# Graph layer behind a layer norm: the mean's subtraction and the clipping done by GpSimd, with a third input buffer

## The chip, the core and the metric

One core of a Trainium2 chip runs the whole program. The metric is the device time of one execution in microseconds (us), the median over several runs. Engines are named as in the profile's rows: PE is TensorE, DVE VectorE, ACT ScalarE, POOL GpSimd, SP SyncE.

## The reference

`x` has 128 matrices of 120 x 1024, `adj` is a symmetric 120 x 120 matrix. Cut to what matters:

```python
h = jnp.maximum(_layernorm(x, axis=-1), 0.0)
Ln = dinv[:, None] * Lap * dinv[None, :]          # from adj
_, U = jnp.linalg.eigh(Ln)
agg = jnp.einsum('vn,bvd->bnd', U, h)
out = relu(agg @ W1 + b1) @ W2 + b2
# non-local block: th, ph, g projections, max pooling by 2,
# softmax(theta phi) g, projection wo, batch norm, residual -> z
return x + einsum('nv,bvd->bnd', U, z) + z
```

`_layernorm` divides by the root of the variance, which is positive, so clipping can come ahead of the division. The kernel works with `max(x - mean, 0)`, multiplies it by `W1`, and applies the factor `rstd` to the product later.

## The kernel before, in words

There are two parts. The first, the setup, holds two pieces of work that run at the same time. The second is a loop over the 128 matrices with the attention, paced by TensorE; it starts when the setup is done and is not touched by the change.

**The eigenvectors.** A 120 x 120 matrix is brought to tridiagonal form by 118 reflections (`reflect` on VectorE, L983, and on TensorE, L694). Of each, GpSimd does five operations on single numbers in `shift` (L429: a sign, a root by a power, a product, a gate). They wait for the vector `u` that VectorE writes in L1015 of the reflection before (`u_ready`) and for its norm (`s2_ready`). The product of L436 (`du_ready`) lets VectorE go on at L990. Then VectorE alone computes eigenvalues and eigenvectors (`minors` and `count`, L1066 to L1110, three times, and a recurrence at L1157 to L1168). Once, at L1122, it waits for a small product of TensorE (L760, `grid_count`). VectorE's last instruction of the setup is L1274 (`setup_done`), which waits for all of `P1` too. Meanwhile the reflections are put together to a matrix in 19 pieces (`factor` on ScalarE, L555, and TensorE, L719; `masked` on GpSimd, L443).

**The normalised matrices.** For each of the 128 matrices: SP loads it into one of two buffers `xin` (`load`, L325); ScalarE sums it with the factor -1/D (`b_sum`, L509), clips `x - mean` at zero into `frelu` (`b_relu`, L514), and squares and sums for the variance (`b_sq`, L519). TensorE transposes `frelu` in eight pieces (`transposes`, L663), ScalarE copies them out of PSUM (`b_ft`, L524), TensorE multiplies by `W1` (`product`, L674), ScalarE keeps the product in `P1` (`b_p1`, L531). On GpSimd, `rstds` (L459) turns the sums of squares into `rstd`, in two halves of 64 matrices.

**The order.** Each engine has one queue, written out by hand. TensorE's part of a matrix is cut into six pieces (`norm_piece`, L685): two of transposes, four of the product of the matrix two before. Reflection `k` is followed by pieces up to number `(k - 2) * 39 // 10`, so that 448 are done with the last reflection; the rest, up to 780, follow without reflections between them. The small product of L760 stands ahead of piece 546 (`GRID_AT * 6`), and `factor` begins at matrix 93. ScalarE goes in slots (`slot`, L535): clear and square matrix `k`, copy the transposes of `k - 2`, sum `k + 1`, keep the product of `k - 4`. At the end GpSimd sets the first row of `xt` to zero (L475, `xt_free`); SP waits for that before its four small loads (L338, L339), and TensorE waits for these ahead of the loop (L898). The root of the sum of squares of the eigenvectors is taken by GpSimd in L469.

Of the kernel before, what the change touches and what calls it, by code (L numbers as in the profile page):

```python
# [46 lines left out]
def build(nc, x, adj, W1, b1, W2, b2, g_w, g_b, th_w, th_b, ph_w, ph_b, wo_w, wo_b,  # L47
          bn_gamma, bn_beta, bn_mean, bn_var, out):
    ctx = ExitStack()
    with ctx:  # L50
# [6 lines left out]
        def sem(name):  # L57
            return ctx.enter_context(nc.semaphore(name))
# [21 lines left out]
        rstd = sb("rstd", [128, B])  # L80
# [4 lines left out]
        with early:  # L85
            def eb(name, shape, dt=F32):
                return sb(name, shape, dt, early)
            xin = eb("xin", [N, 2, D])
            frelu = eb("frelu", [N, 2, D])
            junkx = eb("junkx", [N, D], BF16)  # L90
            fT = eb("fT", [128, 2, KC * N])
            W1s = eb("W1s", [128, KC, H])
            lns = eb("lns", [N, 2, 1])
            QA = eb("QA", [N, 2 * N])
            strict = eb("strict", [N, N])
            sub = eb("sub", [N, N])
# [67 lines left out]
            wyA, wyB = xt[:, 0, :], xt[:, 1, :]  # L164
            part = lambda t, i: t[:, i * 128:(i + 1) * 128]
            wyC, wyCT, wyG, wyL, wyX, wyY, wyP, wyM = [part(wyA, i) for i in range(8)]
            wyS = part(wyB, 0)


        pst = sb("pst", [128, 2, H])  # L170
# [46 lines left out]
        grid_below = sem("grid_below")  # L217
        grid_count = sem("grid_count")
        xcol_ready = sem("xcol_ready")
        x_in = [sem(f"x_in{i}") for i in range(2)]  # L220
        mean_done = sem("mean_done")
        relu_done = sem("relu_done")
        sq_done = sem("sq_done")
# [37 lines left out]
        def late(eng, s, count):  # L261

            if not isinstance(count, int) or count > 0:
                eng.wait_ge(s, count)

        def rounds(eng, lo, hi, body):

            assert (hi - lo) % 2 == 0
            with eng.Fori(lo // 2, hi // 2) as i:
                body(i * 2, 0)  # L270
                body(i * 2 + 1, 1)
# [29 lines left out]
        def _(sp):  # L301
            sp.dma_start(LA[:, 0:N], adj).then_inc(adj_in, 16)
            n = 0
# [18 lines left out]
            sp.dma_start(P1[N:N + 1, :].rearrange("a (b j) -> a b j", j=H),  # L322
                         b1.rearrange("(a c j) -> a c j", a=1, c=1).to_broadcast([1, B + 1, H])).then_inc(b1_in, 16)

            def load(k, par):  # L325

                late(sp, sq_done, k - 1)
                sp.dma_start(xin[:, par, :], x[bass.ds(k, 1), :, :].rearrange("a n d -> n (a d)")).then_inc(x_in[par], 16)
            load(0, 0)
            load(1, 1)  # L330
            rounds(sp, 2, B, load)


            sp.wait_ge(consts, 1)
# [46 lines left out]
        def _(pool):  # L381
# [44 lines left out]
            pool.wait_ge(dve_out, 1)  # L426
            pool.tensor_tensor(colA[:, 6:7], colA[:, 5:6], colA[:, 10:11], ALU.pow).then_inc(pool_out, 1)

            def shift(k):  # L429

                pool.wait_ge(u_ready, k + 1)
                chain(pool.tensor_scalar(sc[:, SGN:SGN + 1], u[:, 1:2], 0.0, 2.0, ALU.is_ge, ALU.mult))
                chain(pool.tensor_scalar(sc[:, SGN:SGN + 1], sc[:, SGN:SGN + 1], -1.0, None, ALU.add))
                pool.wait_ge(s2_ready, k + 1)
                chain(pool.tensor_tensor(sc[:, ROOT:ROOT + 1], sc[:, S2:S2 + 1], sc[:, 11:12], ALU.pow))  # L435
                pool.tensor_tensor(sc[:, DU:DU + 1], sc[:, SGN:SGN + 1], sc[:, ROOT:ROOT + 1], ALU.mult).then_inc(du_ready, 1)  # L436
                pool.tensor_scalar(sc[:, GATE:GATE + 1], sc[:, XN:XN + 1], TINY, -1.0, ALU.is_gt, ALU.mult).then_inc(gate_ready, 1)

            for k in range(STEPS):
                shift(k)  # L440


            def masked(level):  # L443
# [9 lines left out]
                pool.affine_select(out=view(wyL), in_=view(wyL), compare_op=ALU.is_ge, fill=0.0, base=size - 1,  # L453
                                   pattern=[[2 * size, blocks], [0, size]], channel_multiplier=-1).then_inc(wy_mask, 1)

            for level in range(7):
                masked(level)

            def rstds(a, z):  # L459

                pool.wait_ge(sq_done, z)
                chain(pool.tensor_scalar(rstd[0:N, a:z], rstd[0:N, a:z], 1.0 / D, LN_EPS, ALU.mult, ALU.add))
                pool.tensor_tensor(rstd[0:N, a:z], rstd[0:N, a:z], colA[:, 10:11].to_broadcast([N, z - a]),
                                   ALU.pow).then_inc(rstd_done, 1)
            rstds(0, B // 2)


# [3 lines left out]
            pool.tensor_tensor(colA[:, 8:9], colA[:, 7:8], colA[:, 10:11], ALU.pow).then_inc(pool_out, 1)  # L471


            pool.wait_ge(wy_ps, WY_P(7) + 1)
            pool.memset(xt[0:1, :, :], 0.0).then_inc(xt_free, 1)  # L475
            rstds(B // 2, B)
            pool.wait_ge(rstd_done, 2)
            pool.wait_ge(setup_done, 1)

# [26 lines left out]

        @block.scalar
        def _(act):
            def b_sum(s, par):  # L509
                act.wait_ge(x_in[par], s * 8 + 16 - 8 * par)  # L510
                act.activation(junkx[:, :], xin[:, par, :], ACT.Copy, scale=-1.0 / D,
                               accum_out=lns[:, par, 0:1]).then_inc(mean_done, 1)

            def b_relu(s, par):  # L514
                act.wait_ge(mean_done, s + 1)
                late(act, tr_done, s - 1)
                act.activation(frelu[:, par, :], xin[:, par, :], ACT.Relu, bias=lns[:, par, 0:1]).then_inc(relu_done, 1)

            def b_sq(s, par):  # L519
                act.wait_ge(mean_done, s + 1)  # L520
                act.activation(junkx[:, :], xin[:, par, :], ACT.Square, bias=lns[:, par, 0:1],
                               accum_out=rstd[0:N, bass.ds(s, 1)]).then_inc(sq_done, 1)

            def b_ft(s, par):  # L524
                act.wait_ge(tr_done, s + 1)
                late(act, w1_done, s - 1)
                for j in range(2):
                    last = act.activation(fT[:, par, j * 4 * N:(j + 1) * 4 * N], ps_T[par][:, j, 0:4 * N], ACT.Copy)
                last.then_inc(ft_done, 1)

            def b_p1(s, par):  # L531
                act.wait_ge(w1_done, s + 1)
                act.activation(P1[0:N, bass.ds(s * H, H)], ps_m[par][0:N, 0:H], ACT.Copy).then_inc(p1_done, 1)  # L533

            def slot(k, par):  # L535
                fixed = isinstance(k, int)
                if not fixed or k < B:
                    b_relu(k, par)
                    b_sq(k, par)
                if not fixed or 0 <= k - 2 < B:  # L540
                    b_ft(k - 2, par)
                if not fixed or k + 1 < B:
                    act.wait_ge(sq_done, k + 1)
                    b_sum(k + 1, 1 - par)
                if not fixed or 0 <= k - 4 < B:
                    b_p1(k - 4, par)

            act.wait_ge(consts, 1)
            b_sum(0, 0)
            def keep(*copies):  # L550

                for out, in_, scale in copies:
# [27 lines left out]
                    act.wait_ge(wy_ps, WY_P(7) + 1)  # L580
                    keep((QA[:, N:2 * N], ps_V[0:N, 128:128 + N], 1.0))

            for k in range(4):
                slot(k, k % 2)
            rounds(act, 4, WY_SLOT, slot)
            for k in range(WY_SLOT, B + 4):
                slot(k, k % 2)
                if k < WY_SLOT + WY_STEPS:
                    factor(k - WY_SLOT)


# [59 lines left out]
        def _(pe):  # L651
# [60 lines left out]
            pe.wait_ge(params, 16 * PARAMS)  # L712
            done = 0
            for k in range(STEPS):
                wanted = max(0, (k - LN_LEAD) * LN_RATE[0] // LN_RATE[1])
                reflect(k, done, wanted)
                done = wanted

# [621 lines left out]
PARAMS = 15  # L1340
XN, S2, ROOT, GATE, SGN, REC, DU, RG, AC = range(9)
LN_RATE, LN_LEAD, LN_BEHIND = (39, 10), 2, 1
GRID_AT = 91
WY_SLOT, WY_STEPS = 92, 19
WY_T, WY_G = 1, 4
# [38 lines left out]
```

## Time and profile before

| | |
|---|---|
| median of 3 runs | 3405.35 us (3404.03 to 3417.64) |
| profiled execution | 3414.81 us |
| its span in the profile | 3412.6 us |
| PE busy | 3235.3 us (95%) |
| DVE busy | 2318.8 us (68%) |
| ACT busy | 2411.8 us (71%) |
| POOL busy | 1942.8 us (57%) |

The profile is of one execution. Durations in it are to be held against its own 3414.81 us. A group of instructions is shown with its line, engine, operation, the tiles it writes and reads, the shapes, the count, then busy time and the mean of one, and the idle time of the engine just before them with what ended it. In a timeline each row has start and length in us; in brackets is how long the engine had been idle, and who released it.

### The profile page before, as it was taken

How to read it: one execution, taken by the hardware profiler on the slowest of the kernel's cores; microseconds unless marked ns; L12 is line 12 of the kernel's file. 1: busy time of each engine (PE TensorE's matmuls, PEld its weight loads, DVE VectorE, ACT ScalarE, POOL GpSimd, SP SyncE). 2: the span in 40 equal slices, each digit the busy share in tenths (PEclk: the TensorE clock that was granted, in tenths of full speed). 3: DMA queues.
4: the chain of work that ended last, by engine and by line, in shares of the span. 5: the costliest groups of instructions: out<-in, count | busy, mean ns of one | idle time of the engine just before them, and what ended most of it. 6: DMA issues, size and time to landing. Idle time of an engine off the chain costs nothing.

```text
span 3412.6 us, 66625 instructions
## 1 busy us (share of the span) xinstructions
PE 3235.3 (95%) x16512; PEld 2604.2 (76%) x16512; DVE 2318.8 (68%) x6125; ACT 2411.8 (71%) x4381; POOL 1942.8 (57%) x2069
## 2 busy tenths in 40 slices
PE   6888887779999999999999999999999999999997
PEld 4777776657777777777777777777777777777775
DVE  5777778976666666666666666666666666666664
ACT  4777889957666666667666666676666666667665
POOL 4333320126666666666666666666666666666665
PEclk9998999989999999999999999999999999999998
DMA  2233334412222222222222222222222222222222
GB/s 79 79 82 82 93 95 114 112 41 65 70 74 77 70 70 76 70 70 70 76 75 70 70 76 70 70 70 76 75 70 70 75 70 70 70 77 74 70 71 69
DMA packets 111579, 256.28 MB, mean 75 GB/s; under 512 B 47500, under 2 KB 49797, under 8 KB 111493
## 3 DMA queue, kind: packets, MB, share of 16 engines
q1 hardware_dynamic: 111493, 255.25, 27.2%
q8 instruction: 40, 0.66, 0.1%
q14 instruction: 46, 0.38, 0.0%
HBM read 190.69 MB, written 63.44 MB: 74 GB/s over the span
## 4 chain that ended last, share of the span: by engine, by line
PE 81%; DVE 11%; POOL 3%; issue 3%; ACT 1%; DVEq 0%; ACTq 0%; POOLq 0%
PE ps_M L781 8%; PE ps_M L782 8%; PE ps_M L783 8%; PE ps_S L858 7%; PE ps_E L781 7%; PE ps_O L781 7%; PE ps_O L783 7%; PE ps_E L782 7%; PE ps_E L783 7%; PE ps_O L782 7%; PE ps_M L842 3%; PE ps_m L680 1%; POOL sc L435 1%; PE ps_S L863 1%; PE ps_M L797 1%
## 5 line engine op out<-in xcount | busy, mean ns | idle before, releaser
L487 POOL TENSOR_TENSOR p_lo<-p,p_hi 128x512 fp32r<-128x512 f32 x1024 | 1374.3, 1342 | 936.0 <-ACT p_hi L639 931.8
L634 ACT ACTIVATE p<-ps_E 128x512 f32<-128x512 f32 x1024 | 613.5, 599 | 333.0 <-PE ps_E L783 307.6
L1324 DVE TENSOR_REDUCE nmx<-ps_S 128x1 f32<-128x512 f32 x1024 | 658.3, 684 | 130.2 <-PE ps_S L858 127.3
L639 ACT ACTIVATE p_hi<-p 128x512 fp32r<-128x512 f32 x1024 | 647.0, 632 | 32.7
L781 PE MATMUL ps_E<-o_hi,Q_hi 123*128 123x512 f32 x1024 | 426.9, 417 | 0.0
L781 PE MATMUL ps_O<-p_hi,v_hi 128*121 128x512 f32 x1024 | 406.9, 397 | 4.6 <-POOL p_lo L487 4.6
L783 PE MATMUL ps_O<-p_lo,v_hi 128*121 128x512 f32 x1024 | 406.3, 397 | 0.0
L782 PE MATMUL ps_E<-o_hi,Q_lo 123*128 123x512 f32 x1024 | 404.2, 395 | 0.0
L783 PE MATMUL ps_E<-o_lo,Q_hi 123*128 123x512 f32 x1024 | 404.0, 394 | 0.0
L782 PE MATMUL ps_O<-p_hi,v_lo 128*121 128x512 f32 x1024 | 403.8, 394 | 0.0
L1304 DVE TENSOR_REDUCE gf<-ps_M 128x256 f32<-128x512 f32 x256 | 177.0, 691 | 261.9 <-PE ps_M L783 261.9
L858 PE MATMUL ps_S<-Q_hi,o_hi 122*128 122x512 f32 x1024 | 347.3, 399 | 2.7 <-DVE nmx L1324 1.5
L494 POOL TENSOR_TENSOR y<-y,acc 121x512 f32<-121x512 f32 x256 | 329.3, 1286 | 13.5 <-DVE y L1332 13.5
L781 PE MATMUL ps_M<-o_hi,Chi 122*128 122x512 f32 (+1 forms) x768 | 313.0, 408 | 2.5 <-DVE o_lo L1289 1.5
L680 PE MATMUL ps_m<-W1s,fT 128*120 128x128 f32 x2048 | 296.9, 292 | 9.6 <-ACT P L533 9.6
L783 PE MATMUL ps_M<-o_lo,Chi 122*128 122x512 f32 (+1 forms) x768 | 302.4, 394 | 0.0
L782 PE MATMUL ps_M<-o_hi,Clo 122*128 122x512 f32 (+1 forms) x768 | 302.1, 393 | 0.0
L680 PEld LDWEIGHTS ps_m<-W1s,fT 128*120 128x120 f32 x2048 | 254.4, 192 | 29.2 <-issue 23.9
L1295 DVE TENSOR_REDUCE phf<-ps_M 128x256 f32<-128x512 f32 x256 | 175.6, 686 | 128.9 <-PE ps_M L783 128.9
L858 PEld LDWEIGHTS ps_S<-Q_hi,o_hi 122*128 122x128 f32 x1024 | 193.2, 189 | 77.7 <-ACT mrow L624 27.0
L606 ACT ACTIVATE o_hi<-ps_M 120x512 fp32r<-120x512 f32 x256 | 153.2, 598 | 138.7 <-PE ps_M L783 138.7
L781 PEld LDWEIGHTS ps_E<-o_hi,Q_hi 123*128 123x128 f32 x1024 | 193.7, 189 | 49.6 <-issue 6.7
(355 smaller groups left out, 6101.3 us busy)
## 6 DMA issues: line engine op xcount, KB each, us to landing
rbc<-r_dram SPq DMA_DIRECT2D x128, 484.0 KB
xin<-in_x_dram SPq DMA_DIRECT2D x128, 480.0 KB, 4.2
xt<-in_x_dram SPq DMA_DIRECT2D x128, 480.0 KB, 5.0
out_dram<-y SPq DMA_DIRECT2D x128, 480.0 KB, 3.8
o_hi<-mrow SPq DMA_DIRECT2D x256, 2.0 KB
dcol<-y SPq DMA_DIRECT2D x128, 4.0 KB, 2.0
r_dram<-rcol SPq DMA_DIRECT2D x128, 4.0 KB, 1.4
W1s<-in_L_gnn_W_dram SPq DMA_DIRECT2D x1, 512.0 KB, 4.1
```

What stands on the lines that cost most here:

```text
L487: pool.tensor_tensor(p_lo[:, c % 4, :], p[:, c % 4, :], p_hi[:, c % 4, :].bitcast(F32), ALU.subtract).then_inc(plo_sb, 1)
L494: pool.tensor_tensor(y[:, par, f], y[:, par, f], acc[:, par, f], ALU.add).then_inc(y_sb, 1)
L634: act.activation(p[:, c % 4, :], ps_E[c % 2][:, :], ACT.Exp).then_inc(p_sb, 1)
L639: act.activation(p_hi[:, c % 4, :], p[:, c % 4, :], ACT.Copy).then_inc(phi_sb, 1)
L680: last = mm(ps_m[par][0:N, 0:H], fT[:, par, c * N:(c + 1) * N], W1s[:, c, :], start=(c == 0), stop=(c == KC - 1))
L781: mm(dst, whi, mhi, start=start, stop=False)
L782: mm(dst, wlo, mhi, start=False, stop=False)
L783: return mm(dst, whi, mlo, start=False, stop=stop)
L858: mm(ps_S[SBANK[c]][:, :], o_hi[0:NA, par, c * 128:(c + 1) * 128], Q_hi[0:NA, par, :], start=True, stop=True).then_inc(S_ps, 1)
L1295: dve.tensor_reduce(phf[:, j * 256:(j + 1) * 256], ps_M[BANK["ph" + piece[2]]][:, :].rearrange("p (m t) -> p m t", t=2), AX.X, ALU.max).th ...
L1304: dve.tensor_reduce(gf[:, j * 256:(j + 1) * 256], ps_M[BANK["g" + piece[2]]][:, :].rearrange("p (m t) -> p m t", t=2), AX.X, ALU.max).then ...
L1324: dve.tensor_reduce(nmx[:, c:c + 1], ps_S[SBANK[c]][:, :], AX.X, ALU.max, negate=True).then_inc(max_sb, 1)
```

## The change

GpSimd computes `max(x + lns, 0)` with one TENSOR_SCALAR (`relu`), where `lns` holds the negative mean. ScalarE's `b_relu` is gone. On GpSimd the operations stand behind `shift(k)` while there are reflections, placed by the count of TensorE's pieces (76 of them), and the 52 others follow, with `masked` between them. `xin` has three buffers, `lns` four columns. A load waits for the square and the clearing of the matrix three before. ScalarE's sum of the next matrix stands ahead of the copies. The loops of SP and ScalarE over matrices are written out. `junkx`, the unused output of the sums, lies in `xt`. The first `rstds` follows the last `relu`, the second stands ahead of the fill of `xt`.

```diff
-            xin = eb("xin", [N, 2, D])
+            xin = eb("xin", [N, 3, D])
-            junkx = eb("junkx", [N, D], BF16)
-            lns = eb("lns", [N, 2, 1])
+            lns = eb("lns", [N, 4])
+            junkx = wyB[0:N, D // 2:D].bitcast(BF16)
...
-            def load(k, par):
-
-                late(sp, sq_done, k - 1)
-                sp.dma_start(xin[:, par, :], x[bass.ds(k, 1), :, :].rearrange("a n d -> n (a d)")).then_inc(x_in[par], 16)
-            load(0, 0)
-            load(1, 1)
-            rounds(sp, 2, B, load)
+            def load(k):
+
+                late(sp, sq_done, k - 2)
+                late(sp, relu_done, k - 2)
+                sp.dma_start(xin[:, k % 3, :], x[k:k + 1, :, :].rearrange("a n d -> n (a d)")).then_inc(x_in[k % 3], 16)
+            for k in range(B):
+                load(k)
...
+            def relu(s):
+
+                pool.wait_ge(mean_done, s + 1)
+                late(pool, tr_done, s - 1)
+                pool.tensor_scalar(frelu[:, s % 2, :], xin[:, s % 3, :], lns[:, s % 4:s % 4 + 1], 0.0, ALU.add,
+                                   ALU.max).then_inc(relu_done, 1)
...
+            cleared = 0
             for k in range(STEPS):
                 shift(k)
+                while cleared < (placed(k) - 4) // 6 + 2:
+                    relu(cleared)
+                    cleared += 1
...
-            for level in range(7):
-                masked(level)
...
+            for s in range(cleared, B):
+                relu(s)
+                if s >= WY_SLOT + 3 and (s - WY_SLOT - 3) % 2 == 0 and (s - WY_SLOT - 3) // 2 < 7:
+                    masked((s - WY_SLOT - 3) // 2)
             rstds(0, B // 2)
...
+            rstds(B // 2, B)
             pool.wait_ge(wy_ps, WY_P(7) + 1)
             pool.memset(xt[0:1, :, :], 0.0).then_inc(xt_free, 1)
-            rstds(B // 2, B)
...
-            def b_relu(s, par):
-                act.wait_ge(mean_done, s + 1)
-                late(act, tr_done, s - 1)
-                act.activation(frelu[:, par, :], xin[:, par, :], ACT.Relu, bias=lns[:, par, 0:1]).then_inc(relu_done, 1)
...
+            def slot(k):
+                if k < B:
+                    b_sq(k)
+                if k + 1 < B:
+                    b_sum(k + 1)
+                if 0 <= k - 2 < B:
+                    b_ft(k - 2, k % 2)
+                if 0 <= k - 4 < B:
+                    b_p1(k - 4, k % 2)
...
+def placed(k):
+
+    return max(0, (k - LN_LEAD) * LN_RATE[0] // LN_RATE[1])
```

## Rows read from the trace of the kernel before

**Rows 1.** Busy time of each engine in stretches, granted TensorE clock, DMA share, GB/s

```profile
20.00:482.00 462.00, 401.69 (x2936) 335.44 (x2935) 339.17 (x2121) 334.73 (x601) 167.89 (x590) 0.94 0.31 82
482.00:549.00 67.00, 49.22 (x402) 43.98 (x401) 53.33 (x238) 66.61 (x124) 0.00 (x0) 1.00 0.43 111
```

**Rows 2.** Timeline, one reflection: start us, us, engine, line, operation [idle before <-releaser]

```profile
256.99 0.24 POOL L432 TENSOR_SCALAR sc<-u 1x1 f32<-1x1 f32 x1 [2.67 <-DVE u L1015]
...
258.47 0.15 DVE L990 TENSOR_TENSOR u<-sc,u 1x1 f32<-1x1 f32 x1
258.52 0.22 POOL L437 TENSOR_SCALAR sc<-sc 1x1 f32<-1x1 f32 x1
...
258.87 0.20 DVE L997 SCALAR_TENSOR_TENSOR sqj<-u,zw 1x63 f32<-1x63 f32 x1
...
260.71 0.24 POOL L432 TENSOR_SCALAR sc<-u 1x1 f32<-1x1 f32 x1 [1.98 <-DVE u L1015]
```

**Rows 3.** GpSimd's L432: its group (busy, mean ns | idle before), its last start

```profile
L432 POOL TENSOR_SCALAR sc<-u 1x1 f32<-1x1 f32 x118 | 29.2, 247 | 256.3 <-DVE u L1015 253.5 <-DVE u L979 2.8
...
478.61 0.21 POOL L432 TENSOR_SCALAR sc<-u 1x1 f32<-1x1 f32 x1 [1.67 <-DVE u L1015]
```

**Rows 4.** Timeline of ScalarE, one slot after the reflections

```profile
700.92 1.07 ACT L511 ACTIVATE junkx<-xin 120x1024 bf16<-120x1024 f32 x1
...
702.12 1.17 ACT L517 ACTIVATE frelu<-xin,lns 120x1024 f32<-120x1024 f32 x1
...
703.18 1.15 ACT L521 ACTIVATE junkx<-xin,lns 120x1024 bf16<-120x1024 f32 x1
...
705.21 1.07 ACT L511 ACTIVATE junkx<-xin 120x1024 bf16<-120x1024 f32 x1
```

**Rows 5.** Timeline of VectorE at L1122

```profile
549.21 0.22 DVE L1122 SCALAR_TENSOR_TENSOR pv<-ps_up,pv 120x1 f32<-120x1 f32 x1 [9.27 <-PE ps_up L760]
```

**Rows 6.** GpSimd's groups: fills, one-input and two-input operations

```profile
L494 POOL TENSOR_TENSOR y<-y,acc 121x512 f32<-121x512 f32 x256 | 329.3, 1286 | 13.5 <-DVE y L1332 13.5
...
L397 POOL MEMSET o_hi<- 32x2048 f32 x1 | 1.8, 1799 | 0.1
...
L397 POOL MEMSET Q_hi<- 32x1024 f32 x1 | 0.9, 946 | 0.1
...
L462 POOL TENSOR_SCALAR rstd<-rstd 120x64 f32<-120x64 f32 x2 | 0.5, 252 | 0.2
```

**Rows 7.** VectorE late beside GpSimd, first and last of eight; L1076: ns min/median/max

```profile
565.81 0.25 DVE L1082 TENSOR_TENSOR SP<-ST,SM 120x48 f32<-120x48 f32 x1
565.70 0.70 POOL L453 TENSOR_SCALAR_AFFINE_SELECT xt<-xt 128x64 f32<-128x64 f32 x1
...
613.71 0.24 POOL L462 TENSOR_SCALAR rstd<-rstd 120x64 f32<-120x64 f32 x1
613.72 0.29 DVE L1076 TENSOR_TENSOR ST<-SA,SP 120x48 f32<-120x48 f32 x1
...
L1076 DVE TENSOR_TENSOR ST<-SA,SP x177: 200/208/288, 491.1 to 635.1; 120x48 f32<-120x48 f32 x177
```

**Rows 8.** GpSimd begun behind VectorE, in the attention loop

```profile
1014.74 1.23 DVE L1332 TENSOR_TENSOR y<-y,rbc 121x1024 f32<-121x1024 f32 x1 [0.24 <-DMA rbc<-r_dram]
1015.51 1.60 POOL L487 TENSOR_TENSOR p_lo<-p,p_hi 128x512 fp32r<-128x512 f32 x1 [0.80 <-ACT p_hi L639]
```

**Rows 9.** GpSimd's power operation and a two-input operation of VectorE inside it

```profile
716.07 10.54 POOL L463 TENSOR_TENSOR rstd<-rstd,colA 120x64 f32<-120x64 f32 x1
...
724.73 1.22 DVE L1262 TENSOR_TENSOR W2lo<-W2f,W2hi 128x1024 fp32r<-128x1024 f32 x1
```

**Rows 10.** End of the setup: SP's last small load, its landing, the first matmul

```profile
717.61 0.60 SPq L339 DMA_DIRECT2D o_lo<-b2lo  x1
...
728.83 0.75 PE L797 MATMUL ps_M<-Uaug,pst 121*128 121x120 f32 x2 [3.50 <-POOL pst L482]
...
DMA to landing us min/median/max: 2.0/2.0/2.0
```

More of the change, by code:

```diff
@@ L219, in build @@
         xcol_ready = sem("xcol_ready")
-        x_in = [sem(f"x_in{i}") for i in range(2)]
+        x_in = [sem(f"x_in{i}") for i in range(3)]
         mean_done = sem("mean_done")
@@ L508, in _, with b_sum, b_sq @@
         def _(act):
[L509 to L512, printed above, removed]
-            def b_relu(s, par):
-                act.wait_ge(mean_done, s + 1)
-                late(act, tr_done, s - 1)
-                act.activation(frelu[:, par, :], xin[:, par, :], ACT.Relu, bias=lns[:, par, 0:1]).then_inc(relu_done, 1)
-            def b_sq(s, par):
-                act.wait_ge(mean_done, s + 1)
-                act.activation(junkx[:, :], xin[:, par, :], ACT.Square, bias=lns[:, par, 0:1],
-                               accum_out=rstd[0:N, bass.ds(s, 1)]).then_inc(sq_done, 1)
+            def b_sum(s):
+                act.wait_ge(x_in[s % 3], (s // 3 + 1) * 16)
+                late(act, sq_done, s)
+                late(act, relu_done, s - 3)
+                act.activation(junkx, xin[:, s % 3, :], ACT.Copy, scale=-1.0 / D,
+                               accum_out=lns[:, s % 4:s % 4 + 1]).then_inc(mean_done, 1)
+            def b_sq(s):
+                act.wait_ge(mean_done, s + 1)
+                act.activation(junkx, xin[:, s % 3, :], ACT.Square, bias=lns[:, s % 4:s % 4 + 1],
+                               accum_out=rstd[0:N, s:s + 1]).then_inc(sq_done, 1)
             def b_ft(s, par):
@@ L533, in b_p1 @@
                 act.activation(P1[0:N, bass.ds(s * H, H)], ps_m[par][0:N, 0:H], ACT.Copy).then_inc(p1_done, 1)
[L535 to L546, printed above, removed]
+            def slot(k):
[7 more added lines that the diff above has]
+                    b_p1(k - 4, k % 2)
             act.wait_ge(consts, 1)
-            b_sum(0, 0)
+            b_sum(0)
             def keep(*copies):
@@ L581, in factor @@
                     keep((QA[:, N:2 * N], ps_V[0:N, 128:128 + N], 1.0))
[L583 to L588, printed above, removed]
+            for k in range(B + 4):
+                slot(k)
+                if WY_SLOT <= k < WY_SLOT + WY_STEPS:
                     factor(k - WY_SLOT)
@@ L714, in _ @@
             for k in range(STEPS):
-                wanted = max(0, (k - LN_LEAD) * LN_RATE[0] // LN_RATE[1])
+                wanted = placed(k)
                 reflect(k, done, wanted)
```

## The prediction

> **What bounds the kernel now.** I read the stretches first. Between 20 and 482 us the 118 reflections run, TensorE taking 3.9 sixths of a normalised matrix beside each; from 482 us VectorE goes on alone with the eigenvalues while ScalarE and TensorE finish the other matrices, ScalarE busy 66.6 of 67 us [rows 1]. Behind 728 us lies the attention loop, untouched by the change. ScalarE's share invites the change, so the next question is whether anything waits for ScalarE.
>
> In the reflections nothing does. The timeline of one step shows a loop through VectorE and GpSimd alone: the four small operations of `shift` on GpSimd, then L990 to L1015 on VectorE, whose end releases L432 again, at 260.71 us after 256.99 us a step earlier [rows 2]. GpSimd rests between two shifts: 256.3 us over 118 steps, so 2.17 us each, 1.67 us in the last step [rows 3]. ScalarE is beside this loop.
>
> After 482 us ScalarE sets the pace of the matrices, one per 4.29 us (L511 at 700.92 and at 705.21), yet VectorE's own chain ends the setup. It waited for the matrices at one place, L1122: TensorE reached the small product of L760 only when 91 matrices were through, and VectorE stood for 9.27 us [rows 4, 5]. That is all of ScalarE's lateness that the end feels.
>
> **Part by part.** *ScalarE loses the clearing.* From L517's start to L521's is 1.06 us, so its slot falls from 4.29 to 3.23 us [rows 4]. After the last reflection 448 of 546 sixths before L760 are placed, so 16.3 matrices are left; at 3.3 us each they take 54 us and end at 536 us, before the 539.9 us at which VectorE began to wait (549.21 less 9.27) [rows 5]. Gain 9.3 us; the rest of the 52 x 1.06 us = 55 us is hidden by VectorE's chain, which is the next thing late. Were only half the speed-up realised, 3.8 us per matrix would end at 544 us and still save 5 us.
>
> *GpSimd gets 128 clearings*, 76 within the reflections (one in two steps of three, behind the shift, ahead of the next) and 52 after them. No row has this operation. GpSimd's fill of 1024 elements takes 0.946 us, of 2048 1.80 us, so 0.83 ns an element; a TENSOR_SCALAR of 64 takes 0.252 us; together 0.252 + 960 x 0.00083 = 1.05 us. The other end is the two-input form, 1.286 us per 512, so 2.57 us [rows 6]. I take 1.05 us, as it has one input like L462. That fits into GpSimd's rest even in the last step (1.67 us) [rows 3]: as occupation it costs nothing. Its waits (the mean, the transposes of two matrices earlier) were met four steps before by the placement, and it is wanted by TensorE over half a step later; the shift queued behind it, and through it VectorE's L990, is who would pay if not.
>
> *What it does to VectorE* is the large unknown. Between 488 and 645 us I compared the distance between successive starts in VectorE's repeated operations with its median. Eight of them on two SBUF tensors came 0.04 to 0.09 us late, 0.45 us in all, and each lay at the start of a small GpSimd operation that reads SBUF (first 565.81 us beside L453, last 613.72 us beside L462; the usual length is 0.208 us) [rows 7]. There are 16 such GpSimd operations of about 64 elements, as much reading together as one clearing. So a clearing costs VectorE 0.45 us if the misses count, and 0.45 x 16 / 8 = 0.90 us if it always finds VectorE reading two tensors; the whole 1.05 us is the upper end. In the other direction, GpSimd's L487, begun 0.77 us after VectorE's L1332, took 1.60 us, where the like-shaped L494 takes 1.286 [rows 6, 8]: the two do not pass each other freely. The lower end is nothing at all: during GpSimd's power operation of 10.54 us VectorE's two-input L1262 ran its 1.22 us undisturbed [rows 9]. That operation reads 64 elements in ten microseconds, the clearing 1024 in one, so it is nearer to [rows 7]. I take 0.85 us, since a long read always meets a VectorE that is in its chain.
>
> The sum of that: in the reflections the clearing begins behind L437, at 258.8 us in the step shown, and L997 at 258.87 us would be held [rows 2]; 76 x 0.85 = 64.6 us. TensorE's mean granted clock is 0.94 there over 402 us of work, so up to 0.06 x 402 = 24 us of it is work at the lower level [rows 1]; part shows as longer steps, and a longer VectorE chain hides it. I take a third, 8 us off (ends 0 and 24): 56.6. Afterwards 52 clearings, four of them beside reductions and thus free: 48 x 0.85 = 40.8 us.
>
> By the Trainium skill (SBUF — State Buffer, "Who interferes with whom") a VectorE instruction with two SBUF inputs and a GpSimd instruction that reads SBUF exclude each other for a whole instruction; the trace agrees in kind in [rows 7, 8] and not in [rows 9], and by that rule the sum would take 1.05 us per clearing.
>
> *Order at the end.* The second `rstds` now stands ahead of the fill that frees `xt`: L462 and L463 are 0.3 + 10.54 us. The last of SP's four small loads, issued at 717.61 us, lands 2.0 us later, at 719.6; 10.9 us later that is 730.5, against the first matmul's 728.83 [rows 9, 10]. TensorE waits for them: 1.7 us lost. The third buffer, the unrolled loops and `junkx` within `xt` cost nothing: the loads stay beside 4 steps of slack.
>
> Sum: 56.6 + 40.8 - 9.3 + 1.7 = +89.8 us on the profiled execution's 3414.8 us, 3504.6 us. That execution lay 9.5 us above the median of 3405.35 us, so I forecast **3495 us**.
>
> **Rivals.** *(a) The clearing hardly touches VectorE* (up to 0.15 us each), as [rows 9] suggest. Then -9.3 + 1.7 = -7.6 us: 3398 us, up to 3417 at 0.15 us. This is the one that ends not slower. It decides below about 0.2 us per clearing: 128 x 0.2 = 26 us, less 7.6. Chance 0.26.
>
> *(b) VectorE is held for all of each clearing*: 76 x 1.05 + 52 x 1.05 = 134 us, nothing absorbed, -7.6: 3532 us; absorbed as above, some 3515. For it: L487's delay [rows 8]. Against it: [rows 9]. Chance 0.16. It is the rule that the Trainium skill states on the page and in the section named above.
>
> *(c) Partial sharing*, 0.2 to 0.45 us each: 128 x 0.33 - 7.6 = +35, 3440 us. It is [rows 7] with the misses counted. Chance 0.14.
>
> *(d) The clearing is longer than GpSimd's rest.* At 2.57 us it overruns the mean rest of 2.17 us by 0.4 and the 0.1 us of dispatch: 76 x 0.5 = 38 us, less 7.6: 3436 us. Against: one input. Chance 0.05.
>
> *(e) ScalarE's relief matters within the reflections too*, by way of TensorE's queue: up to the 24 us above, so 3374 us. Nothing waits for ScalarE there. Chance 0.03. That the change does not do what it says I give nothing beyond this: the operation is in the diff with its semaphores.
>
> **Numbers.** The forecast has 0.36. A difference of 0.5%, 17 us, is about what a measurement of this kernel can tell. Faster by more: 0.03. Within: (a), 0.27. Slower: the rest, 0.70. The forecast's own range is 3450 to 3515; as (a) must be within, the range is 3396 to 3530 us.
>
> **What would show it.** Right: the last L432 starts some 57 us later than 478.61 us [rows 3]; steps with a clearing about 0.85 us longer than those without, the gap inside VectorE's L995 to L1015; L1122 without a wait; ScalarE idle from about 482 + 56 x 3.3 = 667 us, plus what the reflections grow; the first matmul waiting for the small loads. Wrong: steps of equal length with and without a clearing (then rival a), or L432 waiting for the clearing's end (rival d), or a stretch from the first matmul of the loop to the end of other length than now, 3412.6 - 728.8 = 2683.8 us [rows 10].

## The result, and the profile after

The changed kernel took a median of 3575.17 us (3574.13 to 3576.54, 4 runs), the kernel before in the same session 3411.49 us (3404.03 to 3420.24, 4 runs): a ratio of 1.048, interval 1.045 to 1.051. The forecast was 3495 us, the range ended at 3530 us: right in its sign, short by 80 us. The profiled execution took 3574.13 us, with a span of 3572.3 us, 159.7 us more than the 3412.6 of before.

The page of after, first its busy times, then two of its groups and the chain that ended last:

```profile
PE 3328.0 (93%) x16512; PEld 2692.3 (75%) x16512; DVE 2407.9 (67%) x6125; ACT 2292.2 (64%) x4253; POOL 2437.8 (68%) x2197
...
PEclk9777767996999999999999999999999999999998
...
PE 77%; POOL 11%; DVE 10%; issue 2%; DMA 0%; ACT 0%; POOLq 0%; SPq 0%; DVEq 0%; ACTq 0%
...
L433 POOL TENSOR_SCALAR frelu<-xin,lns 120x1024 f32<-120x1024 f32 x128 | 485.6, 3801 | 13.6 <-PE ps_T L673 6.4
```

Look at the last line first. One clearing takes 3.8 us on GpSimd in the mean (3.72 in the median), where I had taken 1.05 and bounded it at 2.57. GpSimd's busy time rises by 2437.8 - 1942.8 = 495 us, ScalarE's falls by 120. GpSimd now has 11% of the chain.

The stretches, cut at the last reflection and at the end of the setup, as in [rows 1]:

```profile
20.00:598.00 578.00, 494.37 (x2911) 418.87 (x2910) 382.53 (x2110) 260.55 (x523) 444.78 (x663) 0.74 0.24 64
598.00:886.00 288.00, 174.44 (x1438) 163.37 (x1438) 261.72 (x1187) 184.36 (x401) 239.64 (x86) 0.87 0.33 88
```

The reflections end near 598 us instead of 482, with GpSimd busy for 445 of 578 us and TensorE's granted clock at 0.74, where [rows 1] had 0.94 (the mean of the stretch; 1 is the level of 2.4 GHz, 0.5 that of 1.2 GHz). A step with a clearing, GpSimd's timeline, and then VectorE's in the same step:

```profile
260.43 0.22 POOL L439 TENSOR_SCALAR sc<-u 1x1 f32<-1x1 f32 x1
...
261.93 0.23 POOL L444 TENSOR_SCALAR sc<-sc 1x1 f32<-1x1 f32 x1
262.25 3.72 POOL L433 TENSOR_SCALAR frelu<-xin,lns 120x1024 f32<-120x1024 f32 x1
265.95 0.22 POOL L439 TENSOR_SCALAR sc<-u 1x1 f32<-1x1 f32 x1
```

```profile
262.26 0.28 DVE L997 SCALAR_TENSOR_TENSOR zw<-row,sc,ps_up 1x72 f32<-1x72 f32 x1
262.46 0.91 DVE L999 SCALAR_TENSOR_TENSOR srow<-u,sc 1x1 f32<-1x1 f32 x1
263.30 0.21 DVE L1001 SCALAR_TENSOR_TENSOR sqj<-u,zw 1x72 f32<-1x72 f32 x1
...
264.82 0.28 DVE L1019 SCALAR_TENSOR_TENSOR u<-cs,zw,rown 1x70 f32<-1x70 f32 x1
```

The next shift (L439, the old L432) starts in the instant in which the clearing ends, with no idle time before it, though VectorE had `u` ready at 265.10. The step is 265.95 - 260.43 = 5.52 us: 3.72 of clearing and 1.80 of shift, both on GpSimd's queue. VectorE is held as well, which means that its operation lasts longer beside one of GpSimd's (L999 takes 0.91 us, 0.20 in steps without a clearing), but it has the time: it is done 0.85 us before GpSimd is. So in this step the holding costs nothing, and the queue all.

L439's group and its last start, as in [rows 3]:

```profile
L439 POOL TENSOR_SCALAR sc<-u 1x1 f32<-1x1 f32 x118 | 27.7, 234 | 89.8 <-DVE u L1019 87.0 <-DVE u L983 2.8
...
596.88 0.22 POOL L439 TENSOR_SCALAR sc<-u 1x1 f32<-1x1 f32 x1
```

The waits between 20 and 598 us (who waited for whom: us in total, times, longest):

```profile
POOL sc L439 <- DVE u L1019: 87.0, 44, 2.9
DVE u L994 <- POOL sc L443: 40.2, 54, 1.8
```

GpSimd waited for `u` 44 times instead of 117. The last reflection began at 596.9 us, 118.3 us later than before's 478.6. Of the 76 clearings 75 lie between the first start at 20.2 and the last. The 75 steps with one took 5.51 to 5.78 us, 5.56 in the mean, and the other 42 took 3.81 in the mean, near the mean of all before, (478.6 - 20.2) / 117 = 3.92. So 75 x (5.56 - 3.92) = 123 us is the loss, less 42 x 0.11 = 5 us that the others gained.

The profiled execution of before was not one of its quickest. The six kernels of the experiments below that have no clearing on GpSimd within the reflections either began the last one at 467.5 to 471.2 us, with the granted clock at 0.97 to 0.99 up to there instead of 0.94. Held against those, the reflections lost 126 to 129 us and not 118.

After the reflections, VectorE's repeated L1080, as in [rows 7] (ns: least, median, most):

```profile
L1080 DVE TENSOR_TENSOR ST<-SA,SP x177: 195/207/1132, 613.4 to 780.3; 120x48 f32<-120x48 f32 x177
```

The timeline: one held operation; the old L1122; the end of the setup and the loop's first matmul, as in [rows 5, 10]:

```profile
615.99 1.04 DVE L1084 TENSOR_TENSOR SM<-E2P,SP 120x48 f32<-120x48 f32 x1
616.95 0.20 DVE L1086 TENSOR_TENSOR SP<-ST,SM 120x48 f32<-120x48 f32 x1
...
673.86 0.22 DVE L1126 SCALAR_TENSOR_TENSOR pv<-ps_up,pv 120x1 f32<-120x1 f32 x1 [0.65 <-PE ps_up L764]
...
884.90 0.06 DVE L1278 MEMSET phf<- 128x1 f32 x1
...
886.86 0.75 PE L801 MATMUL ps_M<-Uaug,pst 121*128 121x120 f32 x2 [5.31 <-DMA o_lo<-b2lo]
```

A clearing holds one VectorE operation, here for 1.04 us instead of 0.20. From the last reflection's start to the setup's end (L1278) it is now 288.0 us; before, 728.1 - 478.6 = 249.5. That is +38.5. The wait of 9.27 us is gone, 0.65 is left of it; the last step's waits for TensorE are 2.8 us longer; so VectorE's own operations must have taken 38.5 + 8.6 - 2.8 = 44.3 us more. Matched one by one with those of the kernel with no clearing on GpSimd and the copies first (below), they did take 44.5 us more: 0.86 for each of 52 clearings. The loop's first matmul starts 1.96 us after the setup's end (before 0.74): +1.2. The loop itself takes 3572.3 - 886.9 = 2685.4 us, +1.6. And ScalarE, one matrix to the next, as in [rows 4]:

```profile
700.21 1.17 ACT L531 ACTIVATE xt<-xin,lns 120x1024 bf16<-120x1024 f32 x1
...
704.08 1.15 ACT L531 ACTIVATE xt<-xin,lns 120x1024 bf16<-120x1024 f32 x1
...
708.37 1.14 ACT L531 ACTIVATE xt<-xin,lns 120x1024 bf16<-120x1024 f32 x1
```

It takes 3.9 and 4.3 us here, and 4.6 in the mean of the eight matrices from 700.21 us on, where `masked` stands between the clearings; the forecast had 3.23, and before it was 4.29. The matrices now come at the pace of GpSimd, which clears in 3.72 us and masks between.

The four parts, 118.3 + 38.5 + 1.2 + 1.6, make 159.6 us, and the spans differ by 159.7.

### The profile page after: what moved, and what is told of

Same layout as the page of the kernel before. It is cut to its first block, busy times and chain, and to the rows that moved or that the text cites. A ratio compares the mean times of both kernels' runs of the same rounds, so it can differ in the third digit from the quotient of the medians.

```text
span 3572.3 us, 65955 instructions
## 1 busy us (share of the span) xinstructions
PE 3328.0 (93%) x16512; PEld 2692.3 (75%) x16512; DVE 2407.9 (67%) x6125; ACT 2292.2 (64%) x4253; POOL 2437.8 (68%) x2197
## 4 chain that ended last, share of the span: by engine, by line
PE 77%; POOL 11%; DVE 10%; issue 2%; DMA 0%; ACT 0%; POOLq 0%; SPq 0%; DVEq 0%; ACTq 0%
PE ps_M L785 8%; PE ps_M L786 7%; PE ps_M L787 7%; PE ps_S L862 7%; PE ps_E L785 7%; PE ps_O L785 7%; PE ps_E L786 7%; PE ps_O L787 7%; PE ps_E L787 7%; PE ps_O L786 7%; POOL frelu L433 6%; PE ps_M L846 3%; POOL sc L442 1%; DVE ST L1080 1%; PE ps_m L684 1%
## 5 line engine op out<-in xcount | busy, mean ns | idle before, releaser
L433 POOL TENSOR_SCALAR frelu<-xin,lns 120x1024 f32<-120x1024 f32 x128 | 485.6, 3801 | 13.6 <-PE ps_T L673 6.4
L684 PE MATMUL ps_m<-W1s,fT 128*120 128x128 f32 x2048 | 347.3, 325 | 0.0
L684 PEld LDWEIGHTS ps_m<-W1s,fT 128*120 128x120 f32 x2048 | 302.9, 223 | 11.8 <-issue 6.9
L538 ACT ACTIVATE fT<-ps_T 128x480 f32<-128x480 f32 x256 | 131.1, 563 | 216.4 <-PE ps_m L684 209.4
```

Of the source, the lines that this page charges most:

```text
L433: pool.tensor_scalar(frelu[:, s % 2, :], xin[:, s % 3, :], lns[:, s % 4:s % 4 + 1], 0.0, ALU.add, ALU.max).then_inc(relu_done, 1)
L684: last = mm(ps_m[par][0:N, 0:H], fT[:, par, c * N:(c + 1) * N], W1s[:, c, :], start=(c == 0), stop=(c == KC - 1))
```

## The experiments

The first theory was: the queue of GpSimd costs the +118 us, the holding costs the +38. The rival was that the holding sets both. "Last reflection" below is the last start of the shift's first operation; the ratio is to the kernel before in runs of the same chip.

**No clearing on GpSimd**, all else of the change kept.

```diff
+on_pool = lambda s: False
...
+                if k < B and not on_pool(k):
+                    b_relu(k)
                 if k < B:
                     b_sq(k)
```

> The changed kernel with all 128 clearings back on ScalarE, ahead of the squares; third buffer, written-out loops, order of the sums and of the end stay. If the clearing's place is the whole cause: within 5 us of before (about +2 us from the order at the end), last reflection near 480 us, a wait of 8 to 10 us at L1122's counterpart. If the third buffer, the loops or the order cost something: most of the +160 us stays.

Measured 3419.09 us, 1.0036 (1.0022 to 1.005), last reflection at 471.2, wait for the small product 11.4 us, and another wait where VectorE needs all matrices through:

```profile
DVE Cop L1267 <- PE ps_m L784: 2.6, 1, 2.6
```

The third buffer and the unrolled loops save nothing; something costs a little. The candidate was ScalarE's order, in which the next sum now stands ahead of the copies of the transposes: ScalarE waited 62.3 us for TensorE to free `frelu`, against 28.1 before.

**The copies first again**, as before, on top of that.

```diff
-                if k + 1 < B:
-                    b_sum(k + 1)
                 if 0 <= k - 2 < B:
                     b_ft(k - 2, k % 2)
+                if k + 1 < B:
+                    b_sum(k + 1)
```

> a_none (all clearings on ScalarE, third buffer, written-out loops) with the copies of the transposes ahead of the next sum, as before. If the order on ScalarE made a_none 6 us slower than before from the last reflection to the loop: the stretch shrinks from 255.6 to about 250 us, and the time comes within 5 us of before. If the third buffer or the loops did: no change against a_none.

3406.43 us, 1.0000 (0.9988 to 1.0013); the last reflection to the setup's end 249.8 us instead of 255.6. So the order costs 6 us in that stretch while ScalarE clears (3 us more in the reflections, and some 12 us between the two ratios to before), and the buffers nothing that can be told from 0.13%. What this order costs in the change, where ScalarE does not clear, was not tried.

**The clearings only within the reflections, and only after them.**

```diff
+on_pool = lambda s: s < 76
```

> Only the 76 clearings within the reflections on GpSimd, the 52 later ones on ScalarE. Theory (GpSimd is occupied: 3.72 us of clearing and 1.80 us of shift are one queue): steps with a clearing 5.52 us, last reflection near 597 us, +118 us against before in all. Rival (VectorE is held by GpSimd's reads, and that is the price everywhere): 76 x 0.85 = +65 us.

```diff
+on_pool = lambda s: s >= 76
```

> Only the 52 clearings after the reflections on GpSimd, the first 76 on ScalarE. Theory: reflections as before, end near 480 us; then VectorE is held once per clearing, 52 x 0.9 = +47 us, less 9.3 us at the wait for the small product, +1.7 us at the end: +40 us. If occupation of GpSimd were the whole price: -7.6 us.

The first: 3543.66 us, 1.0393 (1.0376 to 1.041), last reflection 599.6. The second: 3443.24 us, 1.0107 (1.009 to 1.0124), last reflection 467.9 as without a clearing, and 285.7 us from there to the setup's end, 30.1 more than with ScalarE clearing; the wait of 11.4 us fell to 0.7 and that of 2.6 us is gone, so VectorE lost 30.1 + 10.7 + 2.6 = 43.4 us over 52 clearings, 0.83 each. Matched one by one, its operations are 44 us longer. The losses nearly add up: 3543.66 and 3443.24 less 3419.09 make +124.6 and +24.2, together 148.7 against 156.1 for both (measured in another session).

**Fills instead of clearings**, about as long on the queue (four of them, 4.0 us), but reading nothing. The output then lacks the normalised matrices; only the times are read.

```diff
-                pool.tensor_scalar(frelu[:, s % 2, :], xin[:, s % 3, :], lns[:, s % 4:s % 4 + 1], 0.0, ALU.add,
-                                   ALU.max).then_inc(relu_done, 1)
+                for i in range(3):
+                    chain(pool.memset(frelu[:, s % 2, :], 0.5))
+                pool.memset(frelu[:, s % 2, :], 0.5).then_inc(relu_done, 1)
```

> Each clearing replaced by four fills of the same 1024 elements on GpSimd, about 4.0 us that write and read nothing (the output lacks the normalised input). Theory: steps with one 5.8 us, 76 x 0.28 = 21 us more than in the changed kernel up to the last reflection (near 618 us), but VectorE is not held by it afterwards: from the last reflection to the loop about 248 us instead of 287; in all +138 us against before. Rival (VectorE held by anything long on GpSimd): afterwards 287 us again. Rival (only reading costs): near before in all.

3557.5 us, 1.0436 (1.0418 to 1.0453), last reflection 612.0, from there 259.1 us, 18 more than the 241 that the stretch takes with no wait in it (the last experiment). The 75 steps with fills took 5.74 us in the mean. With no reading the reflections are as late as ever: the queue sets them. Behind them the loss mostly goes. VectorE there, the two-tensor operation and two of one tensor (before: 169 ns in the median and 1685 ns):

```profile
L1081 DVE TENSOR_TENSOR ST<-SA,SP x177: 200/208/210, 629.7 to 774.4; 120x48 f32<-120x48 f32 x177
...
L1093 DVE TENSOR_SCALAR SR<-SR x18: 169/626/1028, 634.9 to 775.2; 120x2 f32<-120x2 f32 x18
...
L1111 DVE TENSOR_SCALAR SA<-SP x3: 1685/2043/2045, 668.3 to 777.1; 120x2928 bf16<-120x2928 f32 x3
```

Of the 177 two-tensor operations of this line none was held. TENSOR_SCALARs of VectorE were, by up to 0.86 us, even one of two elements a partition, and so were its copies, 5.9 us of the 20 us by which its operations behind the reflections grew.

**Half of each clearing on ScalarE**, the other 512 elements, with a semaphore of its own.

```diff
-                pool.tensor_scalar(frelu[:, s % 2, :], xin[:, s % 3, :], lns[:, s % 4:s % 4 + 1], 0.0, ALU.add,
+                pool.tensor_scalar(frelu[:, s % 2, 0:512], xin[:, s % 3, 0:512], lns[:, s % 4:s % 4 + 1], 0.0, ALU.add,
```

> GpSimd clears columns 0 to 511, ScalarE columns 512 to 1023 of every matrix. Theory: the half takes about 1.9 us on GpSimd and, with the shift's 1.8 us, fits into the steps of 4.4 to 3.7 us and overruns the late ones a little (5 to 10 us in all); VectorE is held about 0.45 us per half: up to 76 x 0.45 = 34 us in the reflections and 52 x 0.45 = 23 us after them, less 9.3, +1.7: +25 to +55 us. Occupation alone, without holding: about 0 us. If the cost goes with the number of clearings and not with their length: +150 us.

3455.35 us, 1.0145 (1.0126 to 1.0165), last reflection 505.2, then 261.6 us. A clearing of 512 takes 2.03 us in the median, and with the shift 3.9 us, about VectorE's own step: GpSimd is only just the bound. The reflections are 37 us longer than with no clearing on GpSimd, and VectorE's own operations in them 21 us. So 512 elements cost 1.7 us less, 3.3 ns each.

**What makes the clearing slow.** In two kernels, run once each, each matrix took another form in turn. Their output is not the wanted one; only the durations are read. The first:

```diff
+                form = s % 7
+                if form == 0:
+                    last = pool.tensor_scalar(o, x_, m, 0.0, ALU.add, ALU.max)
+                elif form == 1:
+                    last = pool.tensor_scalar(o, x_, m, None, ALU.add)
...
+                elif form == 4:
+                    last = pool.tensor_copy(o, x_)
+                elif form == 5:
+                    last = pool.tensor_tensor(o, x_, x_, ALU.add)
```

> Matrix s uses form s mod 7 on GpSimd: 0 the clearing as it is, 1 the addition of the column alone, 2 the maximum with a constant alone, 3 addition and maximum with two constants, 4 a copy, 5 an addition of two tensors, 6 the clearing of 512 columns (the output lacks the clearing in most). If the second operation makes it long: forms 1 and 2 take about half of 3.72 us, 3 is like 0. If the column operand does: 2, 3 and 4 are short (1 to 2 us), 1 is like 0. If it is the length in elements alone: form 4 is like 0. Form 6: half, 1.9 us. VectorE should be held about 0.85 us by each of the one-input forms if what holds it is the reading of 1024 elements.

> Matrix s uses form s mod 6 on GpSimd: 0 two constants, times and plus; 1 one constant, times; 2 the clearing of 64 columns; 3 the clearing of 256 columns; 4 times and plus on 64 columns; 5 the addition of two different tensors of 512 columns (the output lacks the clearing). If the small row of before (0.252 us for 64 elements) misled because times and plus is a cheaper pair: form 0 well under 3.65 us, form 4 near 0.25 us, form 2 near 0.2 + 64 x 0.0033 = 0.42 us. If it misled because short ones are cheap in any form: form 0 is 3.65 us and forms 2 and 4 both near 0.25 us. Form 3 near 1.05 to 1.15 us either way. Form 5 near the 1.29 us of such an operation in the loop, or 1.0 us if the 1.89 us for 1024 scale.

Medians in us, of 1024 elements where nothing else stands:

```
add a column, clip            3.74    times, plus               1.04
add 0, clip (constants)       3.63    times, plus, 64 elements  0.24
add a column alone            2.88    add, clip, 512 elements   2.03
clip alone                    2.79    add, clip, 256 elements   1.16
times alone                   2.80    add, clip, 64 elements    0.54
copy                          1.04    two tensors added         1.89
                                      same, 512, two tensors    1.27
```

Of all one-input forms with arithmetic, "times, plus" is the one quick pair, as quick as a copy; one operation alone takes 2.8 us. The row from which I took the price, L462 of [rows 6], is of that very pair.

The first of the two kernels also shows when VectorE is held. GpSimd's timeline and the long ones of VectorE's beside it:

```profile
617.82 3.70 POOL L442 TENSOR_SCALAR frelu<-xin 120x1024 f32<-120x1024 f32 x1 [0.68 <-ACT xt L541]
618.06 0.92 DVE L1095 TENSOR_TENSOR ST<-SA,SP 120x48 f32<-120x48 f32 x1
...
620.52 1.02 DVE L1107 TENSOR_SCALAR SR<-SR 120x2 f32<-120x2 f32 x1
621.47 1.03 POOL L444 COPY frelu<-xin 120x1024 f32<-120x1024 f32 x1
...
621.78 0.84 DVE L1109 TENSOR_TENSOR SP<-SP,SR 120x96 f32<-120x96 f32 x1
...
624.70 1.89 POOL L446 TENSOR_TENSOR frelu<-xin 120x1024 f32<-120x1024 f32 x1 [2.20 <-ACT xt L541]
624.71 1.95 DVE L1095 TENSOR_TENSOR ST<-SA,SP 120x48 f32<-120x48 f32 x1
```

A two-tensor operation of VectorE is held until some 1.15 us behind the start of GpSimd's, whether that takes 3.70 us (618.98 less 617.82 is 1.16) or 1.03 (622.62 less 621.47 is 1.15); over all one-input forms of 1024 elements it is mostly 1.04 to 1.2 us; with 512 elements until 0.8 us; with two input tensors until 1.96 us. In the 2.5 us that follow in the long form VectorE is free. Its TENSOR_SCALAR was held once more, from 620.52 to 621.54 us, the end of the clearing.

**The copy's clip.** GpSimd only adds, in a form with two inputs, and ScalarE clips in its copy out of PSUM (clipping and transposing commute).

```diff
+                pool.tensor_tensor(frelu[:, s % 2, :], xin[:, s % 3, :],
+                                   lns[:, s % 4:s % 4 + 1].to_broadcast([N, D]), ALU.add).then_inc(relu_done, 1)
...
-                    last = act.activation(fT[:, par, j * 4 * N:(j + 1) * 4 * N], ps_T[par][:, j, 0:4 * N], ACT.Copy)
+                    last = act.activation(fT[:, par, j * 4 * N:(j + 1) * 4 * N], ps_T[par][:, j, 0:4 * N], ACT.Relu)
```

> GpSimd only adds the column, as an addition of two tensors (1.89 us in f_forms against 3.72 us for the clearing), and ScalarE clips while it copies the transposes out of PSUM (Relu for Copy, no more work): the same result with half the occupation of GpSimd. Occupation alone (1.9 + 1.8 = 3.7 us beside steps of 4.4 to 3.4): near before, -8 to +10 us. Theory with the holding (f_forms: this form held VectorE 1.75 us, as two tensors are read): steps with one about 5.5 us, +115 to +130 us up to the last reflection, 52 x 1.7 - 9 = +80 us after it: 3590 to 3620 us, more than the changed kernel although GpSimd works less.

And the same with the quick pair, x times 1 plus the negative mean.

```diff
+                pool.tensor_scalar(frelu[:, s % 2, :], xin[:, s % 3, :], 1.0, lns[:, s % 4:s % 4 + 1], ALU.mult,
+                                   ALU.add).then_inc(relu_done, 1)
```

> GpSimd computes x * 1 + column in one TENSOR_SCALAR (m_forms: times and plus on 1024 elements took 1.045 us), ScalarE clips while it copies the transposes; the same result. This is the change with the duration that the forecast gave it. If holding goes with what is read (0.84 us per 1024 elements of one tensor, whatever the length): GpSimd never late, steps with one 0.7 to 0.8 us longer, last reflection near 525 us instead of 470; after it as in the changed kernel, 288 us less at most 2; 3485 to 3500 us in all. If the holding was tied to the long form (3.72 us): near before, -8 to +20 us. If a column operand takes the pair off its fast way: as l_sum's or the changed kernel's durations, over 3540 us.

With two inputs: 1.89 us a clearing, and 3631.48 us, 1.0652 (1.0628 to 1.0675): half as long on GpSimd, and worse than the change, as VectorE is held for all of it (L999 takes up to 1.93 us in its steps); last reflection 614.7. With the pair: 3524.62 us, 1.0336 (1.032 to 1.0352), 1.12 us in the median, last reflection 557.0, 25 us above the upper end that I had expected of it. This is the kernel that I had priced. In its reflections GpSimd and VectorE show, in one step:

```profile
268.77 1.12 POOL L433 TENSOR_SCALAR frelu<-xin,lns 120x1024 f32<-120x1024 f32 x1
269.00 0.89 DVE L999 SCALAR_TENSOR_TENSOR srow<-u,sc 1x1 f32<-1x1 f32 x1
271.69 0.25 POOL L439 TENSOR_SCALAR sc<-u 1x1 f32<-1x1 f32 x1 [1.80 <-DVE u L1019]
```

GpSimd rests 1.80 us again, and VectorE's 0.7 us is on the path. But the reflections are 557.0 - 467.8 = 89 us longer than in the kernel with no clearing on GpSimd and the copies first. Matched one by one, VectorE's operations in them are 39.7 us longer, 0.52 for each of 76 clearings and not 0.85, and its idle time is 47.8 us longer. Who it waits for there stands in the stretch and the waits within it, first of this kernel and then of the one with no clearing on GpSimd:

```profile
20.00:558.00 538.00, 474.46 (x2919) 402.77 (x2918) 378.42 (x2110) 260.57 (x523) 253.30 (x663) 0.77 0.26 70
```

```profile
DVE row L992 <- PE ps_V L703: 77.7, 116, 1.3
...
DVE xcol L1024 <- PE ps_up L711: 25.0, 42, 1.2
...
PE ps_up L710 <- DVE zw L1013: 54.1, 62, 3.5
```

```profile
20.00:469.00 449.00, 383.47 (x2920) 318.41 (x2919) 337.13 (x2111) 332.24 (x598) 167.46 (x588) 0.97 0.32 84
```

```profile
DVE row L1007 <- PE ps_V L718: 47.1, 117, 1.3
...
DVE xcol L1039 <- PE ps_up L726: 2.9, 6, 0.8
...
PE ps_up L725 <- DVE zw L1028: 48.4, 107, 2.6
```

The granted clock is 0.77 instead of 0.97, TensorE is busy for 474 us with the work that took 383, and VectorE waits 30.6 + 22.1 = 52.7 us more for it. The clock changed between its two levels of 1.2 and 2.4 GHz many times, and TensorE's own part of the step grew. TensorE did not wait for GpSimd's sum here: this profile has no such wait. Nor did it idle for longer in all (538 - 474 = 64 us, 449 - 383 = 66 us before); its waits for `zw` are fewer and longer, 0.87 us in the mean instead of 0.45. By an estimate from these rows, the same work at 0.97 would have left it idle for some 155 of the 538 us. That the longer step makes the clock fall is argued from this and from the change's own 0.74; no run sets the clock by itself.

**The order at the end.** The fill that frees `xt` ahead of the second `rstds`.

```diff
-            rstds(B // 2, B)
             pool.wait_ge(wy_ps, WY_P(7) + 1)
+            pool.wait_ge(sq_done, B)
             pool.memset(xt[0:1, :, :], 0.0).then_inc(xt_free, 1)
+            rstds(B // 2, B)
```

> The changed kernel with the fill that frees xt ahead of the second rstds, as before. Theory: the wait of 5.3 us for the last small load ahead of the first matmul of the loop shrinks to that for the vector operations; 1.7 to 2.5 us less than the changed kernel, near 3573 us. Rival: nothing.

3572.76 us, 1.048 (1.0464 to 1.0496), the change's own ratio; the 2.4 us between the medians are of two sessions and within the noise. The first matmul:

```profile
883.89 0.75 PE L802 MATMUL ps_M<-Uaug,pst 121*128 121x120 f32 x2 [3.49 <-POOL pst L496]
```

It waits for `pst` again and no more for the small load, 0.7 us behind the setup's end (L1279 at 883.15) instead of 1.96.

**The wait at L1122 alone**, in the kernel before: the small product two matrices earlier.

```diff
-GRID_AT = 91
+GRID_AT = 89
```

> The kernel before with the small product ahead of matrix 89 instead of 91. Theory (the wait of 9.27 us was all that ScalarE's lateness cost): 7 to 9 us less than before, the wait of VectorE there near 1 us, everything else the same. Rival: VectorE waits for the matrices or for all of P1 elsewhere, and nothing is gained.

3405.21 us, 0.9994 (0.9985 to 1.0003), nothing that can be told from noise. From the last reflection to the setup's end it takes 245.5 us, 4.0 less than before. The wait goes, and another appears where VectorE needs all matrices through:

```profile
DVE Cop L1248 <- PE ps_m L765: 4.7, 1, 4.7
```

**More matrices beside the reflections**, in the kernel before, which helps at both waits: 40 sixths in ten steps, then 42.

```diff
-LN_RATE, LN_LEAD, LN_BEHIND = (39, 10), 2, 1
+LN_RATE, LN_LEAD, LN_BEHIND = (40, 10), 2, 1
```

> The kernel before with 40 instead of 39 sixths of a matrix for ten reflections (460 instead of 448 sixths done at the last reflection); the small product stays ahead of matrix 91. Theory (h_grid: behind the wait at the small product the end of the matrices is late next, 4.7 us): VectorE waits under 2 us at L1122 and not at L1248, 8 us less from the last reflection to the loop, near 241 us instead of 249.5, for 1 to 3 us more in the reflections: -5 to -8 us. Rival (TensorE's queue sets the steps of the reflections): the reflections grow by as much as the rest shrinks.

```diff
+LN_RATE, LN_LEAD, LN_BEHIND = (42, 10), 2, 1
```

> The kernel before with 42 sixths of a matrix for ten reflections (483 sixths at the last one). Theory: behind the last reflection VectorE waits for nobody any more already in i_rate (240.7 us to the loop), so that nothing is left to gain there; TensorE's 0.2 sixths more per step lengthen the late steps of 3.4 us: 0 to 10 us slower than i_rate. Rival: another gain as from 39 to 40, 8 to 13 us.

3393.86 us, 0.9954 (0.9936 to 0.9972), and 3394.74, 0.996 (0.9946 to 0.9974). The setup's end lies 240.7 and 241.1 us behind the last reflection instead of 249.5, with neither wait left. These two beat the kernel before by 14 us. The stretch accounts for 8.8 of it. The rest goes with the clock in the first of the two: its six executions had a mean granted clock of 0.991 to 0.993 over their whole span, before's in the same session 0.982 to 0.991, and of before's own executions 3402.5 us went with 0.991 and 3419.48 us with 0.982.

## Why the prediction was wrong, step by step

**The price of the clearing is the step that failed**: "0.252 + 960 x 0.00083 = 1.05 us", with 2.57 as the other end. It is 3.72 us. The sum was built of two rows that were each of a quick kind: L462 is "times, plus" and the fill reads nothing, where "add, clip" costs 3.3 ns an element. Neither row had this pair of operations, and I took "one input like L462" as nearness. The upper end came from a two-input form, as if one input could not be slower; it is, 3.7 against 1.9 us for 1024 elements. The kernel that does run at my price (1.12 us) came to 3524.62 us, within the range, though in part by luck: in its reflections VectorE's operations are 40 us longer where I had 64.6, and its idle time is 48 us longer, which I had not foreseen.

**"As occupation it costs nothing"** fell with it. The mechanism is rival (d)'s, which had 0.05, at a price outside its end: the clearing overran GpSimd's rest of 2.17 us by 1.55, and 76 x (3.72 - 2.17) = 118 us, the loss between the two profiles. That it fits to the microsecond is luck, as the rest of 2.17 us is a mean that itself holds some of the time at the lower clock. The fills show it without any reading, the run of half clearings with the overrun nearly gone (+48 instead of +164 us).

**The holding, 0.85 us each, was right in size behind the reflections and wrong in place.** Behind them VectorE's matched operations took 44.5 us more in the change and 44 us in the second split run, 0.86 and 0.85 for each of 52 clearings; the forecast was 40.8 us, as it took four for free. In the reflections the 64.6 us did not appear. The operations there did become 44 us longer, but within time that GpSimd's queue took anyway. They are on the path when the clearing is short, as 40 us. Rival (b)'s rule, also that of the Trainium skill (SBUF — State Buffer, "Who interferes with whom"), agrees in who holds whom: two-tensor operations are held by a GpSimd instruction that reads, and not by fills (none of 177). It differs in how long: in the slow forms not for the whole instruction, but for its first 1.15 us of 3.70; in the quick pair, the copy and the sum of two tensors the two come to the same. [Rows 9], in which a long power operation held nothing, are no contradiction any more: it reads only 64 elements, and clearings of 64 elements lengthened a VectorE operation by 0.08 us at most.

**"I take a third, 8 us off", for TensorE's lower clock, had the wrong sign.** I took work at the lower level as something that a longer VectorE chain hides. In the run with the quick pair the clock was lower instead (0.77, not 0.97), and VectorE waited 52.7 us more for TensorE and 5.5 us less for GpSimd there, which is the 48 us of idle time. In the change itself, GpSimd's queue hides this too. What the lower level had cost before was guessed well: in the run with the small product two matrices earlier, whose reflections are the same code, the last one begins 11 us sooner, at a clock of 0.98.

**The 9.3 us at L1122** went as forecast, but mostly not by ScalarE's relief. TensorE stood ready for the small product and waited for VectorE:

```profile
673.26 0.56 PE L764 MATMUL ps_up<-ones,MJ 120*120 120x1 f32 x2 [8.87 <-DVE MJ L1124]
```

Before, it came straight behind the matrices:

```profile
548.90 0.27 PE L760 MATMUL ps_up<-ones,MJ 120*120 120x1 f32 x2
```

So the matrices were now through at 664.4 us, 67.5 us behind the last reflection, where before it was 548.9 - 478.6 = 70.3: faster by 2.8 us, not by the 13 that the forecast of 536 us meant, since GpSimd paced them. VectorE came to the place 673.2 - 596.9 = 76.3 us behind, before 61.3: the other part of the wait was covered by these 15 us, 13 of them held operations. And by itself the wait was worth only some 4 us of the stretch, as L1248 came next.

**The order at the end** was +1.7; measured +1.2 in the profile, and too little for the medians to tell. **The loop** kept its length to 1.6 us. Two slips change nothing: a shift is five operations, not four, and rival (a) stands with 0.26 and with 0.27.

## What to carry to other kernels

Take the price of an instruction that moves to another engine from a row with the same pair of operations on that engine; where none exists, the range must reach beyond the slowest row (here 2.5 ns an element, and the clearing took 3.6), and the first thing to ask is from what duration on the engine becomes the bound: here 2.17 us, and the price was thought to be under it without a row to show it. An engine that looks idle in a serial loop has only its rest in each step to give, and what it reads is taken from VectorE besides. When a wait is removed, look for the next one before its whole length is counted.

## What the runs showed that I had not expected

- GpSimd's one-input arithmetic on 1024 elements takes 2.8 us with one operation and 3.7 with "add, clip", but 1.04 us with "times, plus", as much as its copy; the sum of two tensors takes 1.89. Why this pair is quick is open.
- GpSimd holds VectorE's two-tensor operations for about as long as its reads would last at the rate of a copy: 1.15 us for 1024 elements, 0.8 for 512, 1.96 for two tensors, counted from its start, whether its own duration is 1.03 or 3.70 us. By VectorE's rows the added time is 0.8, 0.38 and 1.75 us.
- VectorE's TENSOR_SCALARs are held in another way: by fills, which held none of 177 two-tensor operations of one line, and in the last microsecond of a long clearing. That this is GpSimd writing its results is an argument from these two, and was not tried by itself.
- The slower loops went with a lower granted clock of TensorE over the whole stretch (0.74 and 0.77 instead of 0.94 and 0.97), in which its part of each step was longer. What exactly makes the clock fall in one step and not in another stays open, and so does why the higher rate of matrices raised it a little.
